# GpSimd reads the rows of all eight experts ahead of its first write

## The reference

```python
xn = layernorm(x)
# recurrent branch
xc = causal_depthwise_conv(xn, conv_w, conv_b)            # 4 taps
r, i = sigmoid(xc @ W_r.T + b_r), sigmoid(xc @ W_i.T + b_i)
a = sigmoid(log_a) ** (8 * r)
h = scan(h = a * h + sqrt(clip(1 - a * a, 0)) * i * xc)   # along the sequence
attn = rmsnorm(h @ W_out.T) * gamma
# experts: E = 8, capacity 512 tokens each, top 1
probs = softmax(xn @ Wr); eidx = argmax(probs); rank = position within the expert
xe = xn[dispatch]                                          # gather, (8, 512, 128)
ye = relu(xe @ W1[e]) @ W2[e]                              # 128 -> 512 -> 128
y = zeros.at[dispatch].add(ye * p * valid)                 # scatter
out = x + attn + y
```

## Time and profile before

| what | value |
|---|---|
| median of 3 runs | 165.67 us (165.46 to 167.71) |
| the profiled execution | 165.59 us |
| its span, first to last instruction | 163.8 us |
| busy shares | TensorE 76%, VectorE 57%, ScalarE 53%, GpSimd 51% |
| mean granted TensorE clock | 0.878 |

### The profile page before, as it was taken

The page is one execution under the profiler, slowest core; times in us unless marked ns, Lnnn a source line. Parts: engine busy times, 40 slices in busy tenths (PEclk is TensorE's granted clock), DMA queues, the critical chain, the costliest instruction groups (busy, mean ns, idle before and its releaser), DMA issues.

```text
span 163.8 us, 2058 instructions
## 1 busy us (share of the span) xinstructions
PE 124.8 (76%) x684; PEld 98.2 (60%) x684; DVE 93.5 (57%) x207; ACT 86.2 (53%) x197; POOL 83.2 (51%) x102
## 2 busy tenths in 40 slices
PE   5966999999995991699999739896979967941000
PEld 5956999836533890439659318694968956930000
DVE  4179300399898000861512410768948999299990
ACT  3047625014554840648685363999608958635650
POOL 7069640000477774377477876377765807560000
PEclk9997555579999999569999999999999999999555
DMA  4898699970011211011011111011110100116997
GB/s 133 231 270 315 268 356 342 399 318 2 16 48 36 54 58 48 18 49 49 16 52 48 48 48 48 16 50 49 49 46 21 33 16 32 42 58 183 327 301 214
DMA packets 14346, 19.27 MB, mean 118 GB/s; under 512 B 1664, under 2 KB 10112, under 8 KB 14336
## 3 DMA queue, kind: packets, MB, share of 16 engines
q1 hardware_dynamic: 9888, 13.63, 24.5%
q0 software_dynamic: 2048, 4.20, 8.7%
q10 hardware_dynamic: 2400, 1.32, 3.0%
HBM read 10.76 MB, written 8.39 MB: 117 GB/s over the span
## 4 chain that ended last, share of the span: by engine, by line
PE 40%; DVE 24%; DMA 8%; issue 8%; ACT 7%; another core or an unknown queue 6%; POOL 3%; POOLq 1%; SPq 0%; DVEq 0%; ACTq 0%
PE bank L495 8%; PE bank L427 7%; PE bank L385 7%; DVE xnT L869 5%; DMA x_tok<-in_x 4%; PE bank L395 4%; DVE xc L838 4%; PE bank L482 3%; DVE inp L865 3%; PE bank L416 3%; PE bank L484 2%; PE bank L483 2%; DVE dec L922 2%; DMA dec<-y_rows 2%
## 5 line engine op out<-in xcount | busy, mean ns | idle before, releaser
L357 POOL DMA_INDIRECT y_rows<-xn_tok,idx_out x32 | 37.1, 1159 | 25.2 <-DVE xn_tok L876 15.9
L350 POOL DMA_INDIRECT xn_tok<-xn_rows,idx_in x32 | 32.1, 1002 | 29.9 <-DVE idx_out L801 20.4
L618 ACT ACTIVATE h_sb<-bank 128x512 f32<-128x512 f32 x32 | 18.1, 596 | 25.7 <-PE bank L484 16.8
L495 PE MATMUL bank<-w_raw,h_sb 128*128 128x128 f32 x256 | 30.2, 275 | 0.1
L495 PEld LDWEIGHTS bank<-w_raw,h_sb 128*128 128x128 f32 x256 | 29.2, 192 | 0.2 <-issue 0.2
L482 PE MATMUL bank<-xg_hi,w_hi 128*128 128x512 f32 x32 | 14.0, 437 | 12.0 <-ACT h_sb L618 5.4
L427 PE MATMUL bank<-xc,par 128*128 128x512 f32 x32 | 17.2, 670 | 3.0 <-issue 2.8
L845 DVE TENSOR_TENSOR xg_lo<-bank,xg_hi 128x512 fp32r<-128x512 f32 x8 | 5.5, 688 | 18.6 <-ACT xg_hi L612 14.2
L876 DVE COPY xn_tok<-bank 128x512 f32<-128x512 f32 x7 | 4.8, 684 | 18.2 <-remote 11.3
L482 PEld LDWEIGHTS bank<-xg_hi,w_hi 128*128 128x128 f32 x32 | 6.1, 191 | 14.9 <-ACT h_sb L618 6.8
L427 PEld LDWEIGHTS bank<-xc,par 128*128 128x128 f32 x32 | 6.6, 214 | 12.0 <-issue 11.0
(11 more groups left out here) (111 smaller groups left out, 211.8 us busy)
## 6 DMA issues: line engine op xcount, KB each, us to landing
w_raw<-in_weights SPq DMA_DIRECT2D x8, 512.0 KB, 7.5
y_rows<-sca SPq DMA_DIRECT2D x4, 512.0 KB, 5.8
dec<-y_rows SPq DMA_DIRECT2D x8, 256.0 KB, 5.0
x_tok<-in_x SPq DMA_DIRECT2D x3, 512.0 KB, 9.4
xn_rows<-xn_tok SPq DMA_DIRECT2D x3, 512.0 KB, 3.5
out<-dec SPq DMA_DIRECT2D x4, 256.0 KB, 3.0
out<-dec ACTq DMA_DIRECT2D x4, 256.0 KB, 3.2
x_tok<-in_x SPq DMA_DIRECT2D x2, 256.0 KB, 5.4
```

The source lines that it names most:

```text
L350: g.indirect_dma_start(gathered[:, s * D:(s + 1) * D], None, xn_rows, bass.IndirectOffsetOnAxis(ap=idx_in[:, s:s + 1], axis=0)).then_inc(g ...
L357: g.indirect_dma_start(y_rows, bass.IndirectOffsetOnAxis(ap=idx_out[:, s:s + 1], axis=0), gathered[:, s * D:(s + 1) * D], None).then_inc(s ...
L495: last = mm(tile_of(e, s), h_sb[:, k * CAP + s * P:k * CAP + (s + 1) * P], w_raw[:, e, F + k * D:F + (k + 1) * D], start=(k == 0), stop=(k ...
L618: a(h_sb[:, k * CAP:(k + 1) * CAP], hbank[n % 3][:, :], ACT.Relu).then_inc(h_done, 1)
```

## The change

GpSimd's program is reordered. The gathers of all eight experts come first, then the two waits, then the scatters of all eight experts. Count, size and source of the transfers stay, and the programs of the other engines don't change.

```diff
             pool.wait_ge(xn_out, 16 * NU)
             pool.wait_ge(tp_done, NH)
             pool.wait_ge(idx_done, 1)
-            AHEAD = 4
-            for e in range(AHEAD):
+
+            for e in range(E):
                 gather(e)
             pool.wait_ge(idx_done, 2)
             pool.wait_ge(zero_out, 16 * C)
             for e in range(E):
                 scatter(e)
-                if e + AHEAD < E:
-                    gather(e + AHEAD)
```

## The result

The changed kernel took 184.2 us (183.73 to 184.93, 4 runs), the kernel before beside it 165.87 us (165.46 to 167.71, 4 runs). The ratio is 1.126, with an interval of 1.115 to 1.137. The forecast was 165.7 us, no change. Two later comparisons gave 1.131 (1.117 to 1.145) and 1.103 (1.095 to 1.112); in the first of them three of seven runs of the kernel before (164.7 to 167.1 us) and one of four of the changed kernel (186.3 us) were slow ones, and its ratio goes by the others.

The account below looks back on a forecast made before the run. Bound: a latency chain TensorE to ScalarE to VectorE, expert by expert. Span 163.8 us, 0 from gathers, 0 from scatters, plus 1.8 to the profiled execution and 0.08 to the median: 165.7 us, range 164.7 to 167.7 (8 in 10: 162.0 to 172.0).

Parts of the forecast that it names:

- the queue: GpSimd's transfer queue: gathers land as issued and scatters behind them do not queue; priced at nothing, bounded by 1.3 us.
- VectorE's durations: VectorE beside more GpSimd descriptor work from 64 to 84 us: price nothing for the chain, a few tenths per GpSimd instruction.
- the last scatter: End of the kernel: even the slow bound, 143.2 us, leaves the last scatter's issue at 145.52 us.
- the price of nothing: Gathers of experts 4 to 7, moved forward to 64.3 to about 85.1 us: 0 added to the span.
- rival 1: Slower: TensorE's completion signals are held while GpSimd generates descriptors without a pause; 171.4 us, chance 0.26 including the extreme.
- the hold of 7.01 us: Unexplained chain piece before expert 0's eviction at about 66 us in the kernel before; news of finished matmuls came late.
- +21: 186 us: Extreme of rival 1: the first hold lasts until the gathers end, from 66.1 to some 87 us; chance 0.04.
- Rival 2: Faster: fewer gathers from 105 to 122 us remove the 2.68 us hold and a like one earlier; 160.3 us, chance 0.12.

Follow-up runs that it names:

- pause_mid: Changed kernel plus a wait for expert 0's eviction between the gathers of experts 3 and 4: 150.18 us without holds; rerun as pause_mid_2 with holds, 175.47 us.
- ahead6: Kernel before with six experts gathered ahead in place of four, 24 gathers in a row: 150.09 us without holds, 180.4 us with holds.
- plain_all: Changed kernel with all 32 gathers as plain reads of neighbouring rows by GpSimd: 150.58 us beside 150.00 for the kernel before, without holds.
- ahead2: Kernel before with two experts gathered ahead in place of four, eight gathers in a row: 214.72 us beside 161.86 for the kernel before, with holds.

## Why the prediction was wrong

**Where it was right.** The gathers ended at 84.33 (84.2 to 85.1 forecast), and TensorE waited for gathered rows 0.6 us as in the earlier trace rows; the queue, VectorE's durations and the last scatter behaved as priced. A set of four scatters took 5.1 us for expert 0 and 5.9 in the mean of all eight, for the 5.8 forecast. Where nothing was held, kernels with this order or nearly so came within 0.7 us of the kernel before (`pause_mid`, `ahead6`, `plain_all`). That was the forecast's sum, and it was right for the machine that it described.

**The step that failed** is the price of nothing for sixteen indirect gathers beside TensorE, from 64 to 85 us, and with it the weight of rival 1. The prediction saw the hold of 7.01 us, saw that GpSimd's pause at 64.0 stood one to two us ahead of its end, and wrote that the rival "decides once the pause after 64.0 was what released the signals". It gave the case in which the hold lasts with the gathers ("+21: 186 us") a chance of 0.04. The time was 184.2. `pause_mid_2` shows that case: with the pause put back the first hold ends at 65.9 again. The picture of one hold that ends with the row was inexact: the first signal came free at 76.8, inside it, and the last at 94.3, ten us behind it. GpSimd's indirect transfers did not end with the row, though: expert 0's scatters followed up to 89.42 (88.47 + 0.95), and the next signal came at 91.48, 2.1 us after that, as in the kernel before (66.15 after 64.00). A stop of the indirect transfers goes with the release of what is still held; signals that come free inside a row, at 76.8 and 83.8 here, have no such stop, and no rule for them has been shown.

**The argument against the rival** was that GpSimd is busy from 80.3 to 101.8 in the kernel before without a hold of that size. It is true and proved too little. That stretch alternates gathers and scatters; after the change, too, scatters in sets of four with pauses between them held nothing. And small holds were there, in ScalarE's timeline of the kernel before:

```profile
91.04 0.60 ACT L618 ACTIVATE h_sb<-bank 128x512 f32<-128x512 f32 x1 [2.91 <-PE bank L484]
93.15 1.33 ACT L618 ACTIVATE h_sb<-bank 128x512 f32<-128x512 f32 x2 [1.51 <-PE bank L484]
95.31 0.60 ACT L618 ACTIVATE h_sb<-bank 128x512 f32<-128x512 f32 x1 [0.82 <-remote]
...
102.45 0.60 ACT L612 ACTIVATE xg_hi<-bank 128x512 fp32r<-128x512 f32 x1 [1.46 <-remote]
```

These are the relus of expert 3, whose groups had ended at 89.4, 90.1, 90.8 and 92.7, and the copy of transposes that had ended at 99.5: each came 1.6 to 3.1 us late, and all but the last came inside the very stretch that the prediction held against the rival. From the eviction of expert 2 to that of expert 3 the kernel before takes 14.5 us and the changed one 10.6, from expert 4's to expert 5's 8.2 and 5.4. These two differences are about the 6.7 us that the second half gained.

**Rival 2 was right too**, at 6.7 us for its 5.4: with the row of gathers out of it, the second half has no hold at all.

**The base itself.** By the jobs without holds (150.0 to 150.7 us), the 165.87 us of the kernel before contained some 15 us of holds and what followed from them. A trace in which waits end by something unnamed for 6% of the span is one whose next version can't be priced by moving known blocks.

**What stays open.** What holds the signals. The jobs with holds and those without differ in nothing that the kernels do. The traces do differ in what was recorded. In those with holds most completion increments of the gathers are missing: of the 64 for expert 3, the kernel before has 15 and the changed one 17, where `pause_mid` without holds has all 64. Of the 1664 increments of all transfers, the ten traces of jobs without holds have 1661 to 1664, and the nine with holds 1079 to 1336. `ahead2`, which ran in a job with holds but has none, has 1563, and lacks some from expert 0 on. So records go missing in every trace of those jobs, with or without a hold. That points at a rival which no run tests: that the recording is what backs up, and holds TensorE's signals while it does. Then the slowdown would belong to recorded executions of those jobs and not to the kernel. It can't be told here, as every time comes from an execution with recorded spans; a time taken without recording would tell. Whether the changed kernel is as fast as the kernel before in a job without holds was not seen directly.

## What to carry to other kernels

An engine that no one waits for can still set the pace: in the jobs with holds a longer row of its transfers went with later signals of another engine, whatever the cause. Before a row of indirect transfers is made longer, look for waits that end by an unnamed releaser while it runs, and price the case that they last as long as the row. A read-ahead has two cliffs, too little (two experts: an expert pays the circle, 214.7 us) and, where signals are held, too much; four was between them. Filler work that is to keep one engine busy has to be looked at on the others too: sixteen fills of a scratch tile stretched one instruction of VectorE from 0.7 to 10.5 us. And one comparison can be of one machine state: a second job of the kernel before, up to 10% quicker, told more here than any edit.

## What the runs showed of the hardware

An indirect DMA of 128 rows takes GpSimd 0.94 us and 0.30 us until the next, a plain one of the same 64 KB 0.58 us in a row of sixteen. TensorE's completion signals normally reach a waiting engine within 0.1 us of the matmul's end (the four relus of expert 0 started 0.03 us after the ends that the profile gives their groups). In the held state of the changed kernel they came 17 to 32 us late, in order, 2.8 to 7.7 us apart, while ScalarE's own signal was on time (its relu ended at 84.38 and TensorE went on at 84.43). In the kernel before three held ones came together, at 66.15. The Trainium skill, "TensorE: Matmul & The Clock Gate", section "The cost: per-tile semaphore tail", has about 26 ns for each signal; the 0.03 us above don't contradict it, and signals 2.8 to 7.7 us apart are outside it. A hold costs twice: TensorE is idle in it and restarts at the lower clock level (slices 16 to 19 of the clock above), so four gate matmul records took 3.62 us at 85.88 where eight took 3.90 in the earlier trace rows.
